# Second pass of a linear-attention kernel: the router's product moves to another PSUM bank and ahead of the last state products, VectorE's router work ahead of the sparse carries

## The reference

```python
def _layernorm(x, axis=-1, eps=1e-05): ...

def reference(x, w_qkv, w_proj, b_proj, Wq, Wk, Wv, Wqa, Wqb, Wka, Wkb, Wg1a, Wg1b, bg1, Wg2a, Wg2b, bg2, We, Wga, Wgb, norm_w, Wo):
    def attn(x):                       # linear attention, 16 heads of 32
        q, k, v = split(x @ w_qkv.T); q, k = relu(q), relu(k)
        z = 1 / (einsum('bhd,bhdn->bhn', k.sum(-1), q) + eps)
        context = einsum('bhdn,bhen->bhde', v, k)
        return (einsum('bhde,bhen->bhdn', context, q) * z) @ w_proj.T + b_proj
    def chunk_gla(q, k, v, gk, C=64):  # gated linear attention, chunks of 64 tokens
        g = cumsum(gk, axis=1)
        A = tril(einsum('cthd,cshd->chts', q * exp(g), k * exp(-g)))
        ...
        S = S * exp(g_last)[..., None] + chunk_kv      # the state that is carried on
        return A @ v + (q * exp(g)) @ S
    def ffn(x):                        # 8 heads of 64, 4 experts
        q1, k1, v = x @ Wq * scale, x @ Wk, x @ Wv
        q2, k2 = x @ Wqa @ Wqb * scale, softmax(x @ Wka @ Wkb)
        gk1, gk2 = log_sigmoid(x @ Wg1a @ Wg1b + bg1) / 16, log_sigmoid(x @ Wg2a @ Wg2b + bg2) / 16
        e = softmax(x @ We); mask = one_hot(top_1(e))  # the router
        o = chunk_gla(q1, k1, v, gk1) + sum over experts of chunk_gla(q2 * e*mask, k2 * e*mask, v, gk2 * mask)
        g = x @ Wga @ Wgb
        return (o * rsqrt(mean(o*o) + EPS) * norm_w * silu(g)) @ Wo
    x = x + _layernorm(attn(_layernorm(x)))
    return x + _layernorm(ffn(_layernorm(x)))
```

## Time and profile before

| what | value |
| --- | --- |
| median of three runs | 2499.4 us (2497.77 to 2500.72) |
| the profiled execution | 2496.37 us, its span 2494.6 us |
| PE busy | 2397.7 us (96%), 20208 matmuls |
| DVE busy | 1848.0 us (74%) |
| ACT busy | 1554.0 us (62%) |
| POOL busy | 1138.6 us (46%) |
| granted clock of PE | 0.995 of full speed over the span |

### The profile page before, as it was taken

The page is one execution under the profiler, slowest core; times in us unless marked ns, Lnnn a source line. Parts: engine busy times, 40 slices in busy tenths (PEclk is TensorE's granted clock), DMA queues, the critical chain, the costliest instruction groups (busy, mean ns, idle before and its releaser), DMA issues. The chain is left out here.

```text
span 2494.6 us, 56360 instructions
## 1 busy us (share of the span) xinstructions
PE 2397.7 (96%) x20208; PEld 1424.4 (57%) x20208; DVE 1848.0 (74%) x3484; ACT 1554.0 (62%) x3281; POOL 1138.6 (46%) x929
## 2 busy tenths in 40 slices
PE   4999999997999999999999999999999999999997
PEld 1444444454666666666666666666666666666654
DVE  4444444426888888888888888888888888888885
ACT  2322322226777777777777777777777777777773
POOL 1787333313444444444444444444444444444444
PEclk9999999998999999999999999999999999999999
DMA  6434433311111111111111111111111111111111
GB/s 219 102 101 135 102 102 101 84 55 35 42 49 49 43 46 42 42 42 42 42 46 46 50 43 47 42 42 42 42 42 48 45 50 44 44 42 42 42 26 35
DMA packets 250704, 145.65 MB, mean 58 GB/s; under 512 B 208096, under 2 KB 208096, under 8 KB 250144
## 3 DMA queue, kind: packets, MB, share of 16 engines
q1 hardware_dynamic: 240048, 119.32, 19.2%
q10 hardware_dynamic: 9504, 17.31, 1.9%
q0 software_dynamic: 1104, 8.40, 0.9%
HBM read 61.09 MB, written 33.55 MB: 38 GB/s over the span
## 5 line engine op out<-in xcount | busy, mean ns | idle before, releaser
L319 PE MATMUL psum<-wb,region 128*128 128x512 f16 x768 | 293.1, 382 | 0.0
L320 PE MATMUL psum<-wb,region 128*128 128x512 f16 x768 | 292.3, 381 | 0.0
L321 PE MATMUL psum<-wb,region 128*128 128x512 f16 x768 | 292.2, 380 | 0.0
L1056 POOL TENSOR_TENSOR region<-region,kfac 128x512 f32<-128x512 f32 x64 | 66.7, 1042 | 455.5 <-DVE kfac L1309 455.5
L1039 POOL TENSOR_TENSOR region<-region 128x1024 f32<-128x1024 f32 x64 | 147.8, 2309 | 266.2 <-DVE region L1415 233.7
L1415 DVE SCALAR_TENSOR_TENSOR region<-psum,region 128x512 f16<-128x512 f32 x64 | 44.3, 692 | 225.2 <-ACT region L868 225.2
L1044 POOL TENSOR_TENSOR region<-region 128x1024 f32<-128x1024 f32 x64 | 150.5, 2352 | 92.3 <-DVE region L1186 92.3
L1051 POOL TENSOR_SCALAR region<-region,m 128x512 f32<-128x512 f32 x256 | 172.3, 691 | 25.7 <-DVE hm L1257 25.7
L586 PE MATMUL psum<-region 128*128 128x512 f16 x768 | 176.2, 379 | 2.1 <-DVE region L1415 2.1
L1067 POOL TENSOR_TENSOR region<-region,decay 128x512 f32<-128x512 f32 x64 | 67.1, 1048 | 199.0 <-DVE decay L1326 199.0
L1220 DVE SCALAR_TENSOR_TENSOR region<-psum,m,region 128x512 f32<-128x512 f32 x192 | 144.2, 751 | 6.8
(11 more groups left out here) (232 smaller groups left out, 7303.7 us busy)
## 6 DMA issues: line engine op xcount, KB each, us to landing
region<-x_in SPq DMA_DIRECT2D x128, 256.0 KB, 2.6
q_cols<-region ACTq DMA_DIRECT2D x64, 256.0 KB, 2.5
region<-q_cols SPq DMA_DIRECT2D x64, 256.0 KB, 2.8
out_rows<-region SPq DMA_DIRECT2D x62, 256.0 KB, 2.0
region<-wb_in POOLq DMA_DIRECT2D x1, 3072.0 KB, 12.1
region<-wqkv_in SPq DMA_DIRECT2D x4, 512.0 KB, 5.6
region<-region SPq DMA_TRANSPOSE x128, 3.0
region<-ws_in POOLq DMA_DIRECT2D x1, 1280.0 KB, 16.0
```

What stands on the lines that cost most here:

```text
L319: mm(out, lhs(0), rhs(0), start=start, stop=False)
L320: mm(out, lhs(0), rhs(1), start=False, stop=False)
L321: return mm(out, lhs(1), rhs(0), start=False, stop=stop)
```

## The change

Three things are done, all in the second pass. First, `route(n + 1)` writes columns 384 to 387 of bank 1, not of bank 7, and PE runs it inside `state_products`, between the sparse products of head pairs 2 and 3 and those of pairs 0 and 1. Second, the waits move with it: `low_rank` takes over the wait on bank 7's former reader, `project_v` (which writes bank 1 anew) waits for `ldiff_ok`, and `inter_sparse` and `project_k` no longer do. Third, DVE's `front_router` no longer waits for `low1_ok`, and it and `front_label` stand between `back_carry1` and `back_carry`. No arithmetic changes.

```diff
-            def low_rank(n):
+            def low_rank(n, out, join):
+                if out:
+                    pe.wait_ge(S("out_ok"), n - 1)
+                elif join:
+                    pe.wait_ge(S("osum_ok"), n)
...
-            def route(n, out, join):
+            def route(n):
                 pe.wait_ge(S("xnT_in"), n * 16 + 17)
-                if out:
-                    pe.wait_ge(S("out_ok"), n - 1)
-                elif join:
-                    pe.wait_ge(S("osum_ok"), n)
                 for g in range(KT):
-                    last = mm3(bank[7][:, 2 * P:2 * P + NEXP], lambda x: xnT[:, x, g, :], lambda x: wl[:, x, g, 2 * P:],
+                    last = mm3(bank[1][:, ROUTE_AT:ROUTE_AT + NEXP], lambda x: xnT[:, x, g, :], lambda x: wl[:, x, g, 2 * P:],
...
             def project_v(n, first):
                 pe.wait_ge(S("carry1_ok"), prev(n))
+                pe.wait_ge(S("ldiff_ok"), cur(n))
...
             def project_k(n, back):
-                pe.wait_ge(S("ldiff_ok"), cur(n))
...
-            def state_products(n, p, ahead):
+            def state_products(n, p, ahead, more):
...
                 for pr in (2, 3, 0, 1):
+                    if pr == 0 and more:
+                        route(n + 1)
                     if pr == 0 and ahead:
...
                 pe.wait_ge(S("carry_ok"), cur(n))
-                if front:
-                    pe.wait_ge(S("ldiff_ok"), cur(n + 1))
...
-                    state_products(n, p, ahead)
+                    state_products(n, p, ahead, more)
                 if front and more:
-                    route(n + 1, tail, back)
-                    low_rank(n + 1)
+                    low_rank(n + 1, tail, back)
...
             def front_router(n):
                 dve.wait_ge(S("route_pe"), cur(n))
-                dve.wait_ge(S("low1_ok"), cur(n))
-                logits = bank[7][:, 2 * P:2 * P + NEXP]
+                logits = bank[1][:, ROUTE_AT:ROUTE_AT + NEXP]
...
                 if back:
                     back_carry1(m, reset)
-                    back_carry(m, reset)
                 if front:
                     front_router(n)
                     front_label(n)
                 if back:
+                    back_carry(m, reset)
                     back_masks(m)
```

More of the change, by code:

```diff
@@ L24 @@
 EPS_Z = 1.1920928955078125e-07
+ROUTE_AT = 384
 MIX_BANKS = ((4, 5, 6, 7), (1, 2, 3, 4))
@@ L647, in _ @@
             pe.wait_ge(S("mix_f_ok"), 2 * KT)
-            route(0, out=False, join=False)
-            low_rank(0)
+            route(0)
+            low_rank(0, out=False, join=False)
             step(0, 0, 0, back=False, tail=False, first=True)
```

## The result

The changed kernel takes 2513.7 us (median of 4 runs, 2510.89 to 2515.14) against 2499.0 us in the 4 runs of the kernel before that stand beside them. The ratio is 1.006 with a 95% interval of 1.0048 to 1.0073: 0.6% slower. The forecast was 2512.3 us, with a range of 2504 to 2520. The profiled execution has a span of 2509.1 us, against 2494.6; the granted clock is 0.995 in both. In the new kernel L320 to L322 are the old L319 to L321, L473 the old L470, L368 the old L367, L425 the old L424, L491 the old L490 and L500 the old L499; DVE's L1241, L1253, L1256, L1268, L1276 and L1287 are the old L1242, L1254, L1257, L1269, L1277 and L1288.

The account below looks back on a forecast made before the run. PE bounds the kernel: its own work plus a 0.45 us select wait a tile. Switches cost 63 x 0.22 = 13.9 us, less 1 gain: +12.9, 2507.5 on the profiled span, 2512.3 us as median; range 2504 to 2520.

Parts of the forecast that it names:

- The way out, 0.10: PE leaving 128*64 state products for 128*128 matmuls: 0.32 us between starts instead of the 0.217 pair step, 0.10 each.
- The way in, 0.09, and the longer first pair, 0.05: PE going from the router's matmuls back into 128*64 state products: a 0.09 us gap, and 0.05 more for the first pair.
- 0.22 a tile: Cost of the added form switches in PE's state products, 0.78 - 0.57 = 0.21, taken as 0.22 us; bounds 0.10 and 0.49.
- "The two that go gave nothing": PE's waits: the moved ones (`route`, `x1_ok`, `ldiff_ok`) cost nothing, and the two removed had gained nothing.
- The cost does not fall into the wait at L367: At `project_k2`, PE's 0.45 us select wait absorbs none of the 0.22, which counts in full in 63 tiles, 13.9 us.
- The gain of 0.02 a tile: Earlier select on DVE gives PE 0.06, of which `cumulate`'s wait leaves 0.02 us a tile, 1 us in all.
- Room on DVE: Between L1198 and the masks (L1269): 5.26 us of work, masks ready at 1763.93, `label_bc` allowing 1764.19, so 0.26 of room.
- (c): Rival: DVE gets late, 0.2 us a tile beyond its room of 0.26, giving 2525 us; chance 0.06.
- PE's busy time "hardly grows": In the state-product stretch, PE's busy time was to hardly grow, since starts move apart; no size given.
- (a): Rival: the form switch is hidden by weights loaded ahead, only the gain is left, 2498.4 us; chance 0.08.
- (b): Rival: the whole select wait at L367 goes, 27.9 us less 13.9, giving 2485; chance 0.03, with smaller gains.
- (d): Rival: the router's early work wins nothing because `label_bc` holds the masks, 2513 instead of 2512; no separate chance.

Follow-up runs that it names:

- e3: The changed kernel with the router's product cut in two, a pair of state products between the halves; 2527.7 us, ratio 1.0117.
- e1: The changed kernel with the router's product moved ahead of the dense state products, DVE's order kept; 2499.0 us, ratio 1.0002.
- e2: The changed kernel with the router's product made by 24 matmuls of form 128*64 at the same place; 2506.3 us, ratio 1.0034.
- e11: The kernel before with only ACT's small router exponential moved ahead of the first pass over the gates; 2499.2 us, ratio 1.0003.
- e5: e1 with ACT's small router exponential moved ahead of its first pass over the gates; 2495.9 us, ratio 0.9990.
- e4: The changed kernel with DVE's additions back ahead of the router's work, PE's part kept; 2512.8 us, ratio 1.0054.
- e10: e8 with DVE's normalized tokens right behind the query split and ACT's small passes reordered; 2497.5 us, ratio 0.9993.
- e6: e1 with DVE's select made in two halves, PE waiting for one, and DVE's order adapted; 2556.3 us, ratio 1.0231.
- e7: e5's early router exponential and e6's split select together; 2553.2 us, ratio 1.0220.
- e8: e7 with DVE's split of the queries moved ahead of the key sums and the mean square; 2534.9 us, ratio 1.0149.

## Why the prediction was right, point by point

**The way out, 0.10.** Right: 0.32 and 0.32 between the starts, in after and in e3, the same figure that stood in the earlier trace rows.

**The way in, 0.09, and the longer first pair, 0.05.** Right: 0.09 behind the router's 0.16 us matmuls, in after, e1 and e3, though no row of before had a way in behind so short ones. The lower bound (0.03, no way in) and the upper (0.32) are both out. The longest L473 is 430 ns where the median is 379, and PE's L473 in total is 6.4 us longer over 64 tiles, all of it in first pairs.

**0.22 a tile.** 0.237 was measured, and e3 gave 0.242 for another trip. In means over the 46 tiles the terms are 0.10 (a way out in place of a pair step), 0.07 (the way in over the router's own step), 0.05 (the first pair) and 0.01 (the low-rank product behind a way out). Each is the term of the sum to within 0.01; what is over lies in their roundings. In 63 tiles 14.9 us. What the sum took to be all form is not quite that: e2 keeps 0.03 of the longer first pair without a change of form.

**"The two that go gave nothing"; no new wait on PE.** Right. `route`, `project_v` and `low_rank` show none in the waits of PE.

**The cost does not fall into the wait at L367.** Right, and this decided the sign. The wait at L368 is 24.4 in after and in e1, with and without the switch, so the 0.24 was not absorbed by it. e2, e1 and e3 put 0.10, -0.02 and 0.47 into PE's stretch before `label_bc`, and the tile followed each to within 0.01.

**The gain of 0.02 a tile.** This is the term that was mis-sized: the select does start 0.15 behind `inter_sparse` in every one of the 46 tiles (before, 0.19 to 0.22 in most), L368 waits 0.39, and of the 0.06 next to nothing arrived: `gates` to `cumulate` is 9.958 for 9.960 before, so 0.1 us and not 1.2 over the kernel. The step that failed was to take the difference between two single tiles, 11.89 and 11.87, for a rate. In the kernel before two chains end together at `cumulate`. It stands 0.21 to 0.22 behind the matmul ahead of it in 43 of 46 tiles, so PE's own work, with the select's wait in it, holds it; and it starts 0.21 to 0.23 behind the end of L1288 in 45 of them, where the kernels in which that chain visibly holds it have 0.21 to 0.24. Shortening one of the two wins nothing, the select's in e1 (9.955 for 9.960) as little as ACT's in e11 (9.957); shortening both wins 0.043 (e5). The two tiles of rows 2 and 3 could not tell a tie from 0.02. The two errors, 0.02 too little cost and 0.02 too much gain, add up: +14.7 us where +12.9 was forecast.

**Room on DVE.** Forecast 0.26 at the masks, measured 0.44. Rival (c), DVE late by more than its room, did not happen, and e4 shows that even its old order has room left (0.33 a tile). The term that was off is DVE's work, taken as 5.26 us. These rows of after show it at the place where it shrank:

```profile
1769.46 0.15 DVE L1248 TENSOR_REDUCE lab<-lscore 128x1 f32<-128x4 f32 x1
1769.52 1.28 DVE L1207 TENSOR_TENSOR region<-psum,region 128x512 f32<-128x512 f32 x2
1770.71 1.28 DVE L1178 TENSOR_TENSOR region<-psum,cst 128x512 f32<-128x512 f32 x2
```

The additions stand 1.19 ahead of the next row, where before they ran to their full end of 1.29 (DVE then waited for ACT), which is 0.10; and L1207 follows L1248 by 0.06, where L1178 followed the old L1249 by 0.18 (of before: 1761.36 and 1761.54), which is 0.12. Why the rows stand closer here is not shown.

**PE's busy time "hardly grows".** Wrong. It went from 2397.7 to 2414.3 us, by 16.6, though the same 20208 matmuls are made. A PE row lasts to its modelled end and so covers most of a gap between starts; busy time took in all of what the switch costs. On PE neither its idle share nor its busy share tells this kind of loss from work.

**The rivals.** (a), the switch hidden, would have needed under 0.095 a tile. The Trainium skill (TensorE: Matmul & The Clock Gate, Part 2) says that weight loads are pulled ahead of matmuls in flight, and that would have spoken for it. Inside L473 the trace shows it: a pair's weights are loaded 0.21 ahead of its matmuls. Across the way out it doesn't: the first load for the router stands at its matmul's own start, 1766.59, after the loader has idled 0.39.

```profile
1766.59 0.10 PEld L320 LDWEIGHTS psum<-wl,region 128*128 128x128 f16 x1 [0.39 <-issue]
```

On the way in, too, the load of L473's first pair starts with its matmul, at 1766.97, 0.09 behind the router's last. The 128 cycles that the same page of the Trainium skill gives for the drain would make an estimate of 0.11 for two boundaries; the runs show 0.24 for the round trip, and the measurement decides. (b), the whole wait at L367, is what e10 tested directly: with that wait gone entirely, 0.05 a tile against e1 came, and 0.043 of these are the early exp's. (d) was the forecast's own case, and it came true.

## What to carry to other kernels

Count how often TensorE changes the form of its matmuls, as you count waits: a small product in another form put between matmuls of one form cost 0.24 us for each round trip here, no idle time of TensorE and counted as busy, but plain in the distance between starts and in the waits of the weight loads; put it where the form changes anyway. Before you shorten a wait of the bottleneck engine, take the mean over many tiles of the stretch that holds it: where another chain spans the same stretch (here `gates` over ACT and DVE to `cumulate`, 9.95 to 9.96 us in every variant until ACT's part shrank), what you take from the wait comes back a few instructions later, and only shortening both chains wins anything. When you reorder an in-order queue to get at such slack, list every reader behind the moved work first: of five kernels that did so here, four were 1.5 to 2.3% slower, through waits that the trace of before could not show.

## What the hardware showed that I had not expected

**A DVE operation can be held by POOL inside its own row.** Before, DVE's L1254, a TENSOR_SCALAR over 128x4, takes 0.52 us, and in the changed kernel 0.23. Its row in the tile of the earlier trace rows, and POOL's beside it:

```profile
1765.97 0.52 DVE L1254 TENSOR_SCALAR m<-cst,lab 128x4 f32<-128x4 f32 x1
```

```profile
1764.11 2.35 POOL L1044 TENSOR_TENSOR region<-region 128x1024 f32<-128x1024 f32 x1 [1.35 <-DVE region L1186]
```

POOL's addition ends at 1766.46 and L1254 at 1766.49. After, POOL's ends at 1775.62, and L1253 starts there and takes 0.23. In e6 it is L1159, a CAST: 1.32 for 0.43, ending at 1789.28 behind POOL's end at 1788.99, as shown above. It is so in the other tiles too. Before, L1254 starts during POOL's addition in 63 of 64 tiles, takes 0.40 to 0.56 and ends 0.03 behind it, and takes 0.23 in the one other tile; in the changed kernel all 64 take 0.23. In e6, L1159 takes 1.25 to 1.41 in the 61 tiles in which it starts beside L1060, and 0.43 in the other three. So the length of such a row says how long it was blocked, not how much it did. Not every operation is held: L1233 to L1236, which read PSUM, run during the same POOL addition and end before it does. The Trainium skill (SBUF — State Buffer, SBUF: two separate sides) says that DVE and GpSimd share a pair of SBUF ports under an exclusive lock, which whoever starts first keeps for its whole instruction; on DVE's side it names operations in a 2-port mode or with two inputs in SBUF. The rows agree with the lock; in which mode L1254 and L1159 ran, no run here shows. The 0.29 that this takes from the select's forerunners in the kernel before is why its select started 0.21 and not 0.15 behind `inter_sparse`: without it DVE would have been ready in time; over all tiles L1254 lost 17.2 us of busy time by the change, and none of it counted.

**A dependent ACT pass starts 0.03 after its forerunner's end; an independent one 0.10 before it.** L745 starts 1.49 after L751, whose row is 1.46 long, while L740, which doesn't read L751's result, starts 1.36 after it. A small independent operation between two dependent passes cost 0.05 here, and not the 0.18 that its starts span. That is the term that the expectations of e5, e7, e8 and e10 had at 0.18.
